# Four instead of three buffers for the experts' raw weights, and three experts' weights requested at the seam

## The reference: what is computed

```
x = x + tanh(g_xattn) * attention(layernorm(x), ctx, ctx)      # 16 heads of 16
x = x + tanh(g_ffn)   * experts(layernorm(x))

experts: bids = sigmoid(x @ conf.T + b) * wealth               # 8 experts
         each token goes to its two highest bids, weights = softmax of the two
         expert e: down_e( silu(x @ gate_e.T) * (x @ up_e.T) ) # inner width 1024
         the weighted results of the two experts are summed
```

## Time and profile before

| what | value |
|---|---|
| median of three runs | 1198.39 us (1196.59 to 1202.21) |
| the profiled execution's own time | 1202.42 us |
| its span, first to last instruction | 1200.6 us |
| TensorE (PE) busy | 1091.6 us, 91% |
| VectorE (DVE) busy | 668.0 us, 56% |
| ScalarE (ACT) busy | 555.3 us, 46% |
| GpSimd (POOL) busy | 315.6 us, 26% |
| mean granted TensorE clock | 0.961 of full speed |
| weights requested for expert 3, 4, 5, 6, 7 | at 532.5, 545.9, 582.8, 590.6, 873.7 us |

### The profile page before, as it was taken

One profiled execution on the slowest core, in us unless ns is written; L12 is line 12 of the kernel. 1 busy time (PEld: TensorE's weight loads), 2 busy tenths in 40 slices (PEclk: granted clock), 3 DMA queues, 4 the chain that ended last, 5 costly groups with the idle time before them and its releaser, 6 DMA issues. The chain is left out here.

```text
span 1200.6 us, 24032 instructions
## 1 busy us (share of the span) xinstructions
PE 1091.6 (91%) x8213; PEld 896.2 (75%) x8213; DVE 668.0 (56%) x1588; ACT 555.3 (46%) x891; POOL 315.6 (26%) x366
## 2 busy tenths in 40 slices
PE   5789999999999988289899999999989999999994
PEld 4456666666666655247599999999849999999994
DVE  2546777777777774365644444444564444444442
ACT  3456676666676664155533333333453333333331
POOL 2122444444343332311311122112221122112111
PEclk8899999999999997589999999999999999999998
DMA  8100111111111101384621121112141122112111
GB/s 297 52 15 24 39 37 44 48 46 37 37 37 37 44 30 48 121 317 164 220 56 32 22 36 32 28 30 36 31 140 28 22 36 36 31 23 36 32 26 23
DMA packets 48025, 72.85 MB, mean 61 GB/s; under 512 B 6256, under 2 KB 42864, under 8 KB 44912
## 3 DMA queue, kind: packets, MB, share of 16 engines
q0 software_dynamic: 16896, 43.53, 14.2%
q1 hardware_dynamic: 30000, 27.68, 7.8%
q10 hardware_dynamic: 1088, 1.11, 0.3%
HBM read 47.14 MB, written 24.90 MB: 60 GB/s over the span
## 5 line engine op out<-in xcount | busy, mean ns | idle before, releaser
L1519 POOL DMA_INDIRECT out<-y,token x64 | 104.6, 1634 | 473.1 <-DVE y L1453 364.1
L1379 ACT ACTIVATE silu<-gate 128x512 f32<-128x512 f32 x128 | 76.5, 597 | 277.4 <-PE up L1287 277.4
L1299 PE MATMUL down<-w_split,h_hi 128*128 128x512 f32 x512 | 185.9, 398 | 0.0
L901 DVE TENSOR_REDUCE max_neg<-maxps 128x4 f32<-128x1024 f32 x128 | 156.4, 1222 | 52.8 <-PE maxps L510 51.1
L1287 PE MATMUL gate<-x_hi,w_split 128*128 128x256 f32 x1024 | 184.5, 282 | 0.0
L1287 PE MATMUL up<-x_hi,w_split 128*128 128x256 f32 x1024 | 183.8, 281 | 0.0
L1444 DVE TENSOR_TENSOR h<-silu,up 128x512 f32<-128x512 f32 x128 | 88.0, 688 | 171.4 <-ACT silu L1379 171.4
L703 ACT ACTIVATE probs<-scores 128x1024 f32<-128x1024 f32 x124 | 127.8, 1030 | 60.5 <-PE scores L535 60.5
L1287 PEld LDWEIGHTS gate<-x_hi,w_split 128*128 128x128 f32 x1024 | 148.8, 188 | 3.0
L1287 PEld LDWEIGHTS up<-x_hi,w_split 128*128 128x128 f32 x1024 | 147.8, 188 | 0.0
L1301 PE MATMUL down<-w_split,h_lo 128*128 128x256 f32 x512 | 144.2, 282 | 0.0
(11 more groups left out here) (164 smaller groups left out, 1756.3 us busy)
## 6 DMA issues: line engine op xcount, KB each, us to landing
xg<-dispatched SPq DMA_DIRECT2D x41, 272.0 KB, 2.8
stage<-gate_T POOLq DMA_DIRECT2D x8, 1024.0 KB, 7.5
stage<-up_T POOLq DMA_DIRECT2D x8, 1024.0 KB, 9.4
stage<-down_T POOLq DMA_DIRECT2D x8, 1024.0 KB, 12.0
x_all<-x SPq DMA_DIRECT2D x16, 256.0 KB, 6.3
ctxT<-ctxT SPq DMA_DIRECT2D x16, 256.0 KB, 2.7
out<-x_all SPq DMA_DIRECT2D x16, 256.0 KB, 2.1
out<-y,token POOLq DMA_INDIRECT x72, 3.8
```

The lines of the kernel that those rows point to most:

```text
L901: V.tensor_reduce(to, maxps[:], AX.X, ALU.max, negate=True).then_inc(s["max_taken"], 1)
L1299: mm(down[t][:].rearrange("p (n d) -> p n d", n=2), h_hi[:, i, rows], split[:, :, cols], start=i == 0, stop=False, skip_group_check=True)
L1379: nc.scalar.activation(silu[pair % 2][:], gate[pair % 2][:], ACT.Silu).then_inc(s_silu, 1)
L1519: pool.indirect_dma_start(out, bass.IndirectOffsetOnAxis(token[:, t:t + 1], axis=0), y[:, t, :], None, compute_op=ALU.add).then_inc(s_adde ...
```

## The change

One constant is changed: the number of raw-weight buffers.

```diff
@@ -34,7 +34,7 @@
 FIRST = P
 REGION = TOKENS + TILE
-STAGES = 3
+STAGES = 4
 ROW = 272
```

## The result

The changed kernel took 1204.2 us (median of 20 runs, 1199.33 to 1207.87), the kernel before 1199.39 us (20 runs, 1195.94 to 1203.96) beside it. The ratio is 1.0035, with a 95% interval of 1.0023 to 1.0046, so about 4.2 us slower (the two medians lie 4.8 us apart). The forecast was +3.8 us. The profiled execution has a span of 1206.1 us against 1200.6. It is the slowest of the 20 (1207.87 us), so what this one trace shows beyond the forecast need not be typical.

A forecast was written before the change was run, and what follows sets the result against it. TensorE, busy 91% of the span, was taken to bound the kernel. Expert 2's rows +2.7, the clock +1.7 and the vanished collision -0.64 us gave +3.8 on 1198.39, so 1202.2 us; range for 8 in 10: 1196 to 1207.

The forecast's parts named there:

- Nobody waits for weights, so no gain: TensorE never waits for a DMA into `stage`, so a fourth buffer brings no direct gain.
- GpSimd's own time is 0: Three more requests at the seam, 0.54 us each, fit in GpSimd's idle 18.06 us; cost 0.
- Expert 1's rows are not delayed: At the seam, rows asked for at 514.8 still land 10.1 us later, sharing the engines with the weights; 0 us more.
- rival 1: At the seam, expert 1's rows queue behind all weights and land 7.7 us later; 1207.0 us in all; chance 0.11.
- Expert 2's rows, 2.7 us: Asked for at 532.0 beside an unbroken weight stream, they take 8.6 instead of 3.3 us; TensorE's `down` starts 2.7 us later.
- Rival 2, no collision: At the seam, expert 2's rows get through in up to some 6 us, no clock drop; 1197.8 us; chance 0.2.
- The clock, 1.7 us: After TensorE's new idle of about 3.3 us at expert 1, its clock falls to about half; 1.7 us lost, bounds 0 and 1.8.
- The collision that goes, -0.64 us: Expert 7's rows no longer run beside expert 7's weights, so TensorE's wait near 888 us goes; 0.64 us back.
- The wait before expert 6 is not touched: Weights requested at 873.73 us do not slow the add VectorE and TensorE wait for (5.4 us); 0 us.
- rival 3: Weights at 873.73 us do slow that add; TensorE's 2.65 us wait and 1.7 us slow clock go; 1193.4 us; chance 0.05.
- The seam's first add, 0 us: Behind expert 3's weights it lands at some 538.5 instead of 536, before VectorE asks for it at 540.7; 0 us.
- The sum: Whole kernel: +2.7 + 1.7 - 0.64 = +3.8 us, giving 1202.2 us against the runs.

The follow-up runs named there:

- seam_alone: Four buffers; against the kernel before, only expert 3's weight request is moved, from first(1) to the seam; 1.0006 (0.9989 to 1.0022) of the kernel before.
- one_third_at_seam: Four buffers; of expert 3's weights only the gate matrix requested at the seam, later requests rearranged, none at first(5); 1.0008 (0.9988 to 1.0027) of the kernel before.
- after: The changed kernel's first measurement and its profiled trace; 1204.2 us, 1.0035 (1.0023 to 1.0046) of the kernel before.
- rows_before: The changed kernel, but GpSimd requests expert 4's weights in first(1) only once expert 2's rows have landed; 1.0027 (1.0009 to 1.0045) of the kernel before.
- after_again: The changed kernel, unchanged, measured and traced a second time; 1.0015 (0.9997 to 1.0032) of the kernel before.
- own_first_four: The changed kernel with own token, weight and y buffers for the tiles of `first`; 1.0003 (0.9983 to 1.0024) of the kernel before.
- end_alone: Four buffers; against the kernel before, only expert 7's weights are requested earlier, in first(4), none at first(5); 0.9999 (0.9980 to 1.0019) of the kernel before.
- clean_requests: Weights requested only once the next rows have landed, none in first(3) and first(5), no own buffers for `first`; 0.9997 (0.9977 to 1.0016) of the kernel before.
- best: Four buffers, own buffers for the tiles of `first`, weights requested only once the next rows have landed; 1193.95 us, 0.9936 (0.9913 to 0.9959) of the kernel before.
- four_old_requests: Four buffers, but all weight requests stay where the kernel before has them; 0.9993 (0.9973 to 1.0013) of the kernel before.
- own_first_three: The kernel before (three buffers) with own token, weight and y buffers for the tiles of `first`; 1.0024 (1.0005 to 1.0043) of the kernel before.

## Why the prediction was right, point by point

- **Nobody waits for weights, so no gain.** Right: no trace shows a wait for `stage`, with two to four experts on their way.
- **GpSimd's own time is 0.** Right: three times 0.54 us, idle 16.52 us behind them.
- **Expert 1's rows are not delayed (rival 1 falls).** Right: 10.1 us again, and TensorE goes on as before (15.13 against 15.18 us from expert 0 to 1).
- **Expert 2's rows, 2.7 us.** Right, slightly too large: 7.7 and 7.9 us instead of 8.6, and a loss of 2.0 us (540.74 against 538.35, less 0.38 us by which this trace was already late). What the prediction leaned on, the unbroken stream with expert 4's weights, was not needed: seam_alone has the same delay without it. The remaining weights of the seam, 3 us of them at the full rate there, suffice, and one_third_at_seam shows the delay go when they go. Whether weights behind the add lengthen it further is not shown: with 2.0 us of full rate left and weights behind (after) the rows took 7.7 us, with 1.8 us and none (rows_before) 6.3.
- **Rival 2, no collision.** It falls with 7.6 to 7.9 us in three traces. The prediction took this rival to be what follows from a rule of the page "DMA: Bandwidth & Descriptors" of the Trainium skill, section "Queues, rings and completion order": a DMA engine drains some 9 to 17 descriptors from one queue before it goes to the next. That step was wrong: the weights have their turns as well. An estimate from that page's figure, if its descriptors are the 8192-byte packets of the weights in the profile: at 410 GB/s over 16 engines, one turn of weights lasts 2.9 to 5.4 us. The delay of the rows, 7.6 to 7.9 us less 3.3, lies within that, so these traces don't speak against the rule; how many packets go in a turn no run here shows.
- **The clock, 1.7 us.** Half right: it fell in the first trace (1.5 us: 16.02 - 12.49 - 2.0) and not in after_again, seam_alone or own_first_four, after waits of 2.48 against 2.59, 2.24 and 2.69 us. So this term was scatter between 0 and 1.5 us that I had entered as a certain 1.7. Whether it has to do with the two measurements' 0.35 and 0.15% is not shown; their intervals overlap.
- **The collision that goes, -0.64 us.** Right in the mechanism: without weights at `first(5)` expert 7's rows took 2.7 to 4.0 us, and nobody waited. In size too large: expert 5 to 7 is 0.43 us shorter in end_alone and 0.33 in after_again.
- **The wait before expert 6 is not touched, rival 3 falls.** Right: with weights behind the add TensorE waits 2.65, 3.03 and 3.07 us, without 2.76, 2.93, 2.93, 3.17, 3.17 and 3.35 us. The two sets overlap. Why the slow clock lasted 6.5 us from gate to gate in after and rows_before and 4.9 to 5.2 in the others with such a wait stays open.
- **The seam's first add, 0 us.** Right: asked for at 531.36, it took 7.3 us instead of 5.1, and no engine waited for it.
- **The sum.** +3.8 us forecast, +4.2 measured; by the table after_again gives only +1.3 and after +5.1 from the first gate on. The direction and the main term are earned. That the size fits this well is partly luck: the stall and the collision that goes make +1.6 us (2.0 less 0.4), the clock term appeared, with 1.5 us, in one trace of four, and the measured +4.2 is larger than the +1.6 for reasons that are only partly known.

## What to carry to other kernels

Before prefetching deeper, ask whether anybody waits for what is prefetched, and which small, late-requested transfer will now run beside it: here 3 MB asked for 20 us earlier made a 272 KB transfer take 7.7 instead of 3.3 us, and the busiest engine wanted its rows 5.3 us after the request. A wait that looks like pure loss can be the cover of a transfer; removing it paid only together with a request plan that keeps big transfers away from the small one. Holding a transfer back without looking at the next one moves the collision.

## What the runs showed of the hardware

- A transfer of rows on the one queue, asked for beside a flow of weights on the other, took 6.3 to 10.9 us against 2.6 to 4.0 us alone. What counts is how long the flow lasts beside it: expert 1's rows took 10.1 us with 6 and with 9 MB asked for ahead of them, but 6.7 and 7.0 us with 3 MB (clean_requests, best).
- TensorE's granted clock after an idle time of 2.2 to 2.7 us fell in one of four traces at expert 1 (after 2.48, not after 2.24, 2.59 and 2.69), but at expert 4 and expert 6 after 2.65 to 3.35 us in every trace with such a wait. Before expert 7 it fell after 2.98 us (best) and not after 2.88 (own_first_four). What tells them apart is not shown.
- TensorE's pause before expert 7, without a releaser, is 1.87, 2.88 and 2.98 us in the three kernels with own buffers. In the others it is 0.40 to 0.63 us (four_old_requests, seam_alone, rows_before) or not there. Long waits ahead of it don't rule it out: own_first_three has it behind one of 4.43 us. Its cause was not tried.
